# First attention with heads 32 partitions apart, fp32 products on four parts of the array, and packed weights

## The reference

```python
def _feature_map(x, fm_w, fm_b):                 # per head of 8: 16 features
    z = jnp.einsum('nshd,ed->nshe', x, fm_w) + fm_b
    return jnp.concatenate([jnp.exp(z), jnp.exp(-z)], axis=-1)
v, k, q = (_feature_map(t, fm_w, fm_b) for t in (v, k, q))       # 16 heads
scores = jnp.einsum('nqhd,nkhd->nhqk', q, k) / jnp.sqrt(jnp.float32(EMBED))
attn = jax.nn.softmax(scores, axis=-1)
out = jnp.einsum('nhql,nlhd->nqhd', attn, v).reshape(N, S, HEADS * EXP_DIM)
return out @ fc_w.T + fc_b
...
x = x + _L0_xattn_ref(ctx, ctx, _layernorm(x), ...)   # the part above
x = x + _L0_ffn_ref(_layernorm(x), ...)               # 8 experts of 64, weighted, dense
x = x + _L1_xattn_ref(_layernorm(x), ctx, ctx, mask, ...)
x = x + _L1_ffn_ref(_layernorm(x), ...)               # top 2 of 8 experts of 512
```

## Time and profile before

| what | us |
|---|---|
| three runs | 460.05, 459.45, 459.58 (median 459.58) |
| span of the profiled execution (the page has no other time of it) | 460.0 |
| TensorE busy | 372.7 (81%) |
| VectorE busy | 252.0 (55%) |
| GpSimd busy | 175.7 (38%) |
| ScalarE busy | 150.5 (33%) |
| mean granted clock of TensorE | 0.857 of full speed |

### The profile page before, as it was taken

The page is one execution under the profiler, slowest core; times in us unless marked ns, Lnnn a source line. Parts: engine busy times, 40 slices in busy tenths (PEclk is TensorE's granted clock), DMA queues, the critical chain, the costliest instruction groups (busy, mean ns, idle before and its releaser), DMA issues.

```text
span 460.0 us, 6601 instructions
## 1 busy us (share of the span) xinstructions
PE 372.7 (81%) x2130; PEld 290.7 (63%) x2131; DVE 252.0 (55%) x708; ACT 150.5 (33%) x267; POOL 175.7 (38%) x211
## 2 busy tenths in 40 slices
PE   3851879999999999699999598414999999999910
PEld 2421758787887884356558487402788888888800
DVE  5999633426465045551353979588355454545414
ACT  2462522323323225221121556110244343444413
POOL 5999980001010010400111511325466666666322
PEclk9987779999899599655999979655799999999965
DMA  5500000000000001500000444100111111112064
GB/s 146 119 1 0 2 0 1 0 1 0 1 2 0 1 0 41 166 1 0 2 0 1 137 118 135 46 1 13 29 47 51 42 49 43 48 43 48 23 171 120
DMA packets 29352, 18.97 MB, mean 41 GB/s; under 512 B 6683, under 2 KB 27055, under 8 KB 29327
## 3 DMA queue, kind: packets, MB, share of 16 engines
q1 hardware_dynamic: 26831, 13.53, 10.6%
q0 software_dynamic: 2496, 5.12, 4.0%
HBM read 13.99 MB, written 4.65 MB: 41 GB/s over the span
## 4 chain that ended last, share of the span: by engine, by line
PE 68%; DVE 23%; DMA 2%; issue 2%; POOL 2%; ACT 1%; SPq 1%; DVEq 0%; ACTq 0%; POOLq 0%
PE ps L1150 58%; PE ps L1573 4%; DVE xn L556 3%; DVE kbhi L624 3%; DVE qlo L630 3%; DVE stats L544 2%; PE ps L1322 1%; DMA dnT<-y_dram 1%; DVE uplo L797 1%; PE ps L1548 1%; DVE x L806 1%; PE ps L1279 1%; DVE mv L547 1%; PE ps L1450 1%; DVE x L962 1%
## 5 line engine op out<-in xcount | busy, mean ns | idle before, releaser
L390 POOL TENSOR_SCALAR rstd<-mv 128x4 f32<-128x4 f32 x16 | 4.0, 251 | 200.6 <-DVE mv L547 200.6
L504 POOL DMA_INDIRECT y_dram<-yb,dst_row x39 | 38.4, 984 | 33.4 <-DVE yb L937 33.4
L640 DVE TENSOR_REDUCE mx<-ps 128x8 f32<-128x616 f32 x32 | 25.6, 799 | 46.3 <-PE ps L1150 46.0
L1042 ACT ACTIVATE ex<-ps 128x512 f32<-128x512 f32 (+1 forms) x40 | 23.9, 597 | 76.4 <-PE ps L1150 76.4
L498 POOL DMA_INDIRECT xg<-xn_dram,src_row x39 | 37.9, 972 | 16.5 <-PE ps L1548 9.3
L1150 PEld LDWEIGHTS ps<-Vx,ex 128*128 128x128 f32 (+1 forms) x320 | 41.7, 201 | 0.9
L1150 PE MATMUL ps<-dnT,hhT 128*128 x312 | 41.4, 276 | 0.6 <-DVE yb L937 0.6
L1150 PE MATMUL ps<-Vx,ex 128*128 128x51 f32 (+2 forms) x320 | 41.5, 278 | 0.0
L1150 PEld LDWEIGHTS ps<-dnT,hhT 128*128 128x128 f32 x312 | 37.9, 192 | 4.1 <-issue 0.8
L1118 ACT ACTIVATE gl<-ps 128x512 f32<-128x512 f32 x39 | 23.3, 597 | 47.0 <-PE ps L1150 47.0
L1150 PE MATMUL ps<-uphi,xghi 128*128 x78 | 35.2, 451 | 0.9 <-DVE xghi L923 0.6
(11 more groups left out here) (262 smaller groups left out, 786.7 us busy)
## 6 DMA issues: line engine op xcount, KB each, us to landing
upn<-in_L_ffn_gate_up_w_dram SPq DMA_DIRECT2D x8, 512.0 KB, 4.2
dnn<-in_L_ffn_down_w_dram SPq DMA_DIRECT2D x8, 256.0 KB, 4.9
dnT<-y_dram SPq DMA_DIRECT2D x8, 256.0 KB, 4.9
x<-in_x_dram SPq DMA_DIRECT2D x4, 256.0 KB, 3.7
xn_dram<-xn SPq DMA_DIRECT2D x4, 256.0 KB, 2.3
out_dram<-x SPq DMA_DIRECT2D x4, 256.0 KB, 2.3
xg<-xn_dram,src_row POOLq DMA_INDIRECT x39, 2.5
y_dram<-yb,dst_row POOLq DMA_INDIRECT x39, 2.2
```

The lines of the kernel that those rows point to most:

```text
L504: g.indirect_dma_start(y_dram, bass.IndirectOffsetOnAxis(ap=dst_row[:, k:k + 1], axis=0), yb[:, k % 2, :], None).then_inc(scattered[k % 2] ...
L640: v.tensor_reduce(mx[:, b % 2, i, half * HH:half * HH + HH].rearrange("p (a h) -> p a h", a=2), ps[:, pair:pair + 2, 0:HK // 2].rearrange( ...
L1042: s.activation(ex[0:rows, m % RING, :], bank[1 + m % 2][0:rows, :], ACT.Exp, scale=SCALE).then_inc(act_ex, 1)
```

## The change

Constants and SyncE first, then the engines. Heads come in 4 groups of 4 per batch, each head on 32 partitions of its own: 16 features, and behind them rows that are 1 since their weights are zero (exp of 0). In `qs` row 16 of each head is overwritten by the negated maximum, which comes by DMA from `mT`. Scores of a head are then one fp32 product of 17 rows into a bank of its own (77 keys by 512 queries); four heads stand on four row parts of the array. Values are one fp32 product per head with 32 columns of weights, four heads on four column parts, all into bank 6; ScalarE copies them to `oT`, TensorE turns them back, VectorE normalises. Maxima still use one fp32r product on all rows, with rounded queries `qh` and spread keys `kb`, 308 columns per product. Weights are laid out ahead of the launch and loaded as `pack0`, `pack1` and `pack2`; `ctx` comes turned. The folding of the second attention's weights moves from set-up to the last batch of the loop.

```diff
-NJ = 2 * NC
-LAG = 2
-RING = 5
-STEPS = NB * NJ + LAG
+RING = 4
+STEPS = NB * NG
+MAX_SPLIT = ((0, 3, 6), (6, 9, 11), (11, 14, 16), (16, 16, 16))
...
+            for b in range(NB):
+                sp.wait_ge(act_mT, b + 1)
+                for g in range(NG):
+                    sp.dma_start(qs[FD:P:R, b, g, :], mT[GH * g:GH * g + GH, b % 2, :]).then_inc(shifted[b % 2][g], 16)
```

GpSimd, set-up:

```diff
+            layernorm_rstd(0, 0)
+            layernorm_rstd(0, 1)
+            g.wait_ge(act_kst, NG)
+            spread_keys(1)
+            layernorm_rstd(0, 2)
+            round_queries(1)
+            layernorm_rstd(0, 3)
```

VectorE, set-up:

```diff
+            layernorm_apply(0, 0)
+            v.wait_ge(act_kst, NG)
+            v.tensor_tensor(kb[:, 0, :, :].bitcast(F32R).rearrange("p g (j k) -> p g j k", j=GH),
...
+            layernorm_apply(0, 1)
+            for n in range(HEADS // 2):
+                max_of(0, n)
+            v.wait_ge(ld_x[2], 16)
+            layernorm_stats(2)
+            for n in range(HEADS // 2, HEADS):
+                max_of(0, n)
+            layernorm_apply(0, 2)
+            v.wait_ge(ld_x[3], 16)
+            layernorm_stats(3)
+            layernorm_apply(0, 3)
```

ScalarE, set-up and loop:

```diff
+            queries(0, qh[:, 0], act_qh)
+            queries(0, qs[:, 0], act_qs)
+            copy_xT(0, 1, bank[6])
+            queries(1, qs[:, 1], act_qs)
...
+                        s.activation(ex[:, p % RING, :, :], ps[0:KEYS, 2 * h:2 * h + 2, :], ACT.Exp, scale=SCALE).then_inc(act_ex, 1)
+                if G >= 1:
+                    copy_oT(G - 1)
```

TensorE, set-up and loop (`NG` is 4 groups, `GH` 4 heads, `R` 32 partitions, `GK` 308, `FD` 16; `Wz` is a part of `pack0`):

```diff
+            def spread(src, cols, n):
+                for g in range(NG):
+                    ins = mm(bank[g][:, 0:n], Wz[R * g:R * g + R, :], src[R * g:R * g + R, cols])
+                return ins
-                mm(o, sel[:, half, cols], nmT[:, b % 2, :], True, False)
-                mm(o, kbhi[:, b, half, cols], qhi[:, b, half, :], False, False)
-                mm(o, kblo[:, b, half, cols], qhi[:, b, half, :], False, False)
-                mm(o, kbhi[:, b, half, cols], qlo[:, b, half, :], False, True).then_inc(pe_sc, 1)
+            def scores(G):
+                b, g = divmod(G, NG)
+                pe.wait_ge(shifted[b % 2][g], 16 * (b // 2 + 1))
+                if G >= 1:
+                    pe.wait_ge(act_ex, 2 * G)
+                else:
+                    pe.wait_ge(act_qs, NG * NB)
+                for j in range(GH):
+                    rows = slice(R * j, R * j + FD + 1)
+                    ins = mm(bank[j][0:KEYS, :], kst[rows, g, b * KEYS:(b + 1) * KEYS], qs[rows, b, g, :])
+                    if j % 2:
+                        ins.then_inc(pe_sc, 1)
+            def values(G):
+                b, g = divmod(G, NG)
+                pe.wait_ge(act_ex, 2 * G + 2)
...
+                for j in range(GH):
+                    ins = mm(bank[6][R * j:R * j + R, :], Vx[:, b, g * P + R * j:g * P + R * j + R],
+                             ex[:, (2 * G + j // 2) % RING, j % 2, :])
+                ins.then_inc(pe_av, 1)
+            for G in range(STEPS + 2):
+                b, g = divmod(G, NG)
+                if G < STEPS:
+                    scores(G)
+                if b + 1 < NB:
+                    for n in range(MAX_SPLIT[g][0], MAX_SPLIT[g][1]):
+                        max_job(b + 1, n)
+                if 1 <= G <= STEPS:
+                    values(G - 1)
+                if G >= 2:
+                    turn_values(G - 2)
...
```

More of the change, by code:

```diff
@@ L21 @@
 HEADS, HD, FD = 16, 8, 16
-HH = HEADS // 2
-HK = HH * KEYS
-NC = -(-HK // P)
+GH = 4
+NG = HEADS // GH
+GK = GH * KEYS
+R = P // GH
 E0, H0 = 8, 64
@@ L54 @@
 LOOP1 = LOOP0 + (NBLK - 1 - LOOP0) // UNROLL * UNROLL
[L57 to L78, removed]
 def two_layer_kernel(nc, A, out):
@@ L425, in _ @@
[L425 to L431, removed]
-                                    wide(kf[:, half, b * KEYS:(b + 1) * KEYS].unsqueeze(1), P, HH, KEYS),
-                                    wide(maskK[:, :].unsqueeze(2), P, HH, KEYS), ALU.mult).then_inc(pool_kbf, 1)
@@ L440, in _ @@
+            layernorm_rstd(0, 0)
[5 more added lines that the diff above has]
+            layernorm_rstd(0, 3)
+            for b in range(2, NB):
+                spread_keys(b)
+            round_queries(2)
             add_bias(0)
@@ new lines, in queries, with copy_mT, copy_oT @@
+            def queries(b, dst, signal):
+                s.wait_ge(pe_z, b + 1)
+                for g in range(NG):
+                    s.activation(dst[:, g, :], bank[g], ACT.Exp, bias=bz[:, 0:1], scale=sgn).then_inc(signal, 1)
+            def copy_mT(b):
+                s.wait_ge(pe_nmT, b + 1)
+                s.activation(mT[:, b % 2, :], bank[4][0:HEADS, :], ACT.Copy, scale=-1.0).then_inc(act_mT, 1)
+            def copy_oT(G):
+                s.wait_ge(pe_av, G + 1)
+                if G >= 2:
+                    s.wait_ge(pe_T, G - 1)
+                s.activation(oT[:, G % 2, :], bank[6], ACT.Copy).then_inc(act_oT, 1)
@@ L1156, in transpose_xn @@
                 ins.then_inc(pe_xT, 1)
+            def spread(src, cols, n):
+                for g in range(NG):
+                    ins = mm(bank[g][:, 0:n], Wz[R * g:R * g + R, :], src[R * g:R * g + R, cols])
+                return ins
+            pe.wait_ge(ld_l0, 16)
+            pe.wait_ge(ld_ctx, 16)
+            spread(ctxT, slice(0, NB * KEYS), NB * KEYS).then_inc(pe_kz, 1)
             pe.wait_ge(pool_ident, 1)
-            pe.wait_ge(ld_ctx, 16)
+            pe.wait_ge(act_kst, NG)
@@ L1231, in turn_nm, with queries @@
-            def turn_nm(b):
-                pe.wait_ge(dve_nm, b + 1)
-                if b >= 2:
+                for g in range(NG):
+                    ins = pe.transpose(bank[4 + b][0:KEYS, g * P:(g + 1) * P], kst[:, g, b * KEYS:(b + 1) * KEYS], ident[:, :])
+                ins.then_inc(pe_vt, 1)
+            def queries(b):
+                pe.wait_ge(xT_ready, b + 1)
+                if b >= 1:
+                    pe.wait_ge(act_qs, NG * b)
+                spread(xnT[:, b, :], slice(0, SEQ), SEQ).then_inc(pe_z, 1)
@@ L1255, in gate_logits, with turn_on @@
-            def gate_logits(b, last):
+                    ins = pe.transpose(bank[7][:, i * P:(i + 1) * P], oT[:, G % 2, i * P:(i + 1) * P], ident[:, :])
+                ins.then_inc(pe_T, 1)
+            def turn_on(b, pair, dst):
+                for i in range(2):
+                    for a in range(2):
+                        at = (2 * i + a) * P
+                        ins = pe.transpose(dst[:, at:at + P], on[:, b % 2, 2 * pair + i, a * P:(a + 1) * P], ident[:, :])
+                ins.then_inc(pe_onT, 2)
@@ L1256, in gate_logits, with project @@
+            def project(b, dst):
+                pe.wait_ge(ld_w, 16)
+                pe.wait_ge(act_onT, (b + 1) * NI)
+                for i in range(NI):
+                    for a in range(2):
+                        ins = mm(dst[:, i * D:(i + 1) * D], onT[:, i, a, :], fcT[:, a, :], a == 0, a == 1)
+                ins.then_inc(pe_fc, 1)
+            def gate_logits(b, last, dst):
                 pe.wait_ge(ld_small, 16 * N_SMALL)
@@ new lines, in _ @@
+            transpose_xn(0, 0, bank[0])
+            queries(0)
+            pe.wait_ge(act_vx, 3)
+            transpose_xn(0, 1, bank[6])
+            queries(1)
+            for n in range(HEADS // 2):
+                max_job(0, n)
+            for n in range(HEADS // 2, HEADS):
+                max_job(0, n)
+            turn_max(0)
+            pe.wait_ge(act_vx, NB)
+            transpose_xn(0, 2, bank[7])
+            queries(2)
+            pe.wait_ge(xT_ready, 2)
+            transpose_xn(0, 3, bank[6])
@@ new lines, in _ @@
+            queries(3)
+            for G in range(STEPS + 2):
+                b, g = divmod(G, NG)
+                if G < STEPS:
+                    scores(G)
+                if b + 1 < NB:
+                    for n in range(MAX_SPLIT[g][0], MAX_SPLIT[g][1]):
+                        max_job(b + 1, n)
+                if 1 <= G <= STEPS:
+                    values(G - 1)
+                if G >= 2:
+                    turn_values(G - 2)
+                if b + 1 < NB:
+                    for n in range(MAX_SPLIT[g][1], MAX_SPLIT[g][2]):
+                        max_job(b + 1, n)
+                    if g == 2:
+                        turn_max(b + 1)
+                if 1 <= b < NB and g >= 2:
+                    pe.wait_ge(dve_on, G - 1)
+                    turn_on(b - 1, g - 2, bank[7])
+                if b >= 2 and g == 0:
+                    pe.wait_ge(dve_on, G - 1)
+                    project(b - 2, bank[7])
+                if b == NB - 1:
+                    fold(g)
+                    if g == 0:
+                        pe.wait_ge(dve_max, HEADS * NB)
+                        transpose_xn(1, 0, bank[5])
+                    elif g == 2:
+                        pe.wait_ge(act_lg, 1)
+                        transpose_xn(1, 1, bank[5])
+                    else:
```

(3 more changed lines are left out.)

708 lines of the change are left out of this document (268 added, 440 removed).

## The result

The changed kernel takes 470.06 us (median of 4 runs, 469.23 to 471.66) against 459.81 for the kernel before on the same chip: ratio 1.0232, 95% interval 1.0203 to 1.0261. It is slower, by 10 us; the forecast was 424. The profiled execution has a span of 468.9.

What follows compares the result with a forecast made beforehand. VectorE's set-up chain to 60.7 us, then TensorE's first attention, were taken as bounds. First score at 41, loop 86 and 5, then 5.2 and 0.3 put the gates' copy at 139.5, 35.4 earlier: 460.0 to 424.6, forecast 424, range 408 to 482.

Steps and rivals of the forecast that it cites:

- The loop: First attention's 16 groups: 48 for twelve, 12.6 around them, 25.6 for the last batch, 86 us, plus 5 for shapes.
- signs of being wrong: Set over 1.9 us, loop clock at 0.5, or first scores after 50 because GpSimd's rounding holds back `rstd`.
- Set of four at 0.96, full overlap: Loop: four fp32 products on different array parts run together in 0.96 us; one after another would be 3.84.
- B: Rival: parts overlap by half, because records start strictly in order; a set takes 2.4 us, kernel 473; chance 0.28.
- C: Rival: no overlap between array parts, 106 us more, 530 or 520 with some on waits; chance 0.09.
- Change of shape, 0 to 0.17 each: Loop: changing array shapes four times a group, 64 in all, costs 0 to 11 us; 5 taken.
- The group, 4.0: Loop: 0.96 scores, 0.96 values, 0.49 transposes and 1.6 maxima make 4.0 us per group of four heads.
- A: The forecast itself: four parts at once, 424 us, own range 408 to 442; chance 0.54.
- D: Rival: four parts at once but loop at half clock, groups of 6.4 instead of 4.0 us, kernel 467; chance 0.09.
- The loop at full clock: From first score at 41 to last normalisation at 134 us, with 5 for changes of shape.
- First score, 41: End of set-up: first score at 41 us, 20 earlier than before, with GpSimd's rounding of at most 5.5 just hidden.
- From the last normalisation to the gates' copy: After the loop: 17 small gate operations and an apply, 5.2, and 0.3 more; copy at 139.5 us.

Runs made afterwards that it cites:

- e6: Changed kernel with heads 0 and 2 of every score and value set left out: 492.74 us, one run.
- e8: Changed kernel with GpSimd's keys and queries after the applies, 36 bf16 fillers before the first score, and scores on 32 rows: 438.44 us, ratio 0.9527.
- e10: e9 with VectorE's small gate operations moved behind the last normalisation and behind the products with batch 0's gates: 426.28 us, ratio 0.9449.
- e5: Changed kernel with GpSimd's spreading and rounding of batches 2 and 3 waiting until VectorE has applied all four batches' normalisation: 476.53 us.
- e9: e8 with one more filler behind each of the first batch's 16 maximum products and four instead of eight before the last transposes: 433.36 us.
- e1: Changed kernel with score products on 32 rows instead of 17, the added rows holding ones: 442.83 us, ratio 0.9591.
- e7: Changed kernel with GpSimd's keys and queries after the applies and 36 bf16 fillers before the first score, scores on 17 rows: 472.31 us, ratio 1.0279.
- e3: Changed kernel with four bf16 filler products on 128 rows ahead of each value set: 460.78 us, ratio 0.999.
- e4: Changed kernel with four bf16 filler products on 17 rows ahead of each value set: 503.69 us, ratio 1.0937.
- e12: e1's kernel timed again, beside the unedited changed kernel (469.6 us) on the same chip: 442.78 us, ratio 0.9777.

## Why the prediction was wrong

The failed step is one premise under **The loop**: the group's prices were taken at full clock. The overlap was right; the clock alone turned the direction. Three of the prediction's signs of being wrong came: a set over 1.9 us, a loop at 0.5, and first scores after 50, though not by the rounding that it named. Point by point, against its sum:

- **Set of four at 0.96, full overlap.** Right: 1.00 to 1.09 at full clock, and e6's two products cost the same. B and C, 0.37 of the chances, are refuted. By the program-order rule that the prediction cited (the Trainium skill, TensorE: Matmul & The Clock Gate, Packing small matmuls) the second record of one part would hold up the next, and a set would take 2.4; the trace disagrees with that, 1.00 for eight records.
- **Change of shape, 0 to 0.17 each.** 1.09 and 1.00 against 0.96 bound it at 0.13, and e8's groups (1.03 and 1.00) at 0.07. If all 64 cost the mean of e8's two excesses, 0.055, they are 3.5 us, an estimate; 5 was taken. The drain of which the Trainium skill speaks (TensorEngine Tiling (Array Packing), Key Properties) costs no more than this at the two changes that lead into a set; the others weren't measured.
- **The group, 4.0.** A group of e8 takes 3.8 at full clock (51.04 to 54.87), one of the changed kernel 6.4 at half (57.30 to 63.66), near the figures of A and D.
- **The clock: +37.1.** From first score to last normalisation: 133.9 in the changed kernel, 96.8 in e8 with the same list at nearly full clock (1.00 to 120 us, 0.93 behind it). D had this, and a chance of 0.09. That its 467 lies so near is in part luck: it has 12 us for half clock in the last four groups, of which three had full clock, and nothing for the late first score. Its evidence was at hand: the earlier trace rows had fp32 products at half clock with TensorE never idle. That busy share does not by itself hold the clock up was written down, and the loop was priced at full clock all the same.
- **The loop at full clock: +3.8.** 96.8 in e8 against the forecast's 93, and this hides two errors. The first twelve groups with what stands around them were forecast at 60.6 and took 60.7 (47.33 to 108.08), and the 5 for changes of shape wasn't needed on top. From there to the last normalisation it is 36.1 against 27.4, 8.7 more: small gate operations, one slowed by GpSimd, stand ahead of the last normalisations; e10 shows 5.9 to be had there. The working looked only behind the last normalisation.
- **First score, 41: +11.0.** GpSimd beside the last apply (e5: 3.3 of it at the first score), then the half clock from 20 us on (e9: another 4.1, with the clock at 0.94). The remaining 3.6 wasn't traced to single steps. GpSimd's rounding, which had been the feared one, was short: 1.89 against at most 5.5.
- **From the last normalisation to the gates' copy: -0.8** (4.7 against 5.5). **Behind it: -6.8.** 278.3 against 285.1 us; the dense layer's half clock lasted 14 us instead of 28, though the apply of 4.94 came again.

11.0 + 37.1 + 3.8 - 0.8 - 6.8 = 44.3, which is 468.9 - 424.6.

## What to carry to other kernels

Packing small fp32 products on parts of the array multiplies the work per time almost fully (four in 1.00 to 1.09 us, one in 0.96), but price it at both clocks before believing the gain: here such a group cost 3.8 or 6.4 us. Use all 32 rows of a part when the added ones leave the result as it is; here they held ones, whose constant the softmax cancels, it cost no time in a set and gave 27 us. Zeros weren't tried. When a step frees an engine, list what its neighbour then starts: GpSimd's wide operations, moved beside VectorE's applies, made one apply 6.4 us longer.

## What the runs showed of the hardware

- In this loop rows in use, not TensorE's waits, decided the clock: 17 rows 0.50, 32 rows 1.00, with equal durations at equal clock (e1, e7, e8); bf16 fillers on 128 rows raised it, on 17 they didn't (e3, e4). Rows that hold nothing but ones count.
- Rows aren't the whole rule. With 17 rows the clock was full for some us behind a projection on 128 rows (121.90) and in the last batch. With products nearly all on 64 to 128 rows, and TensorE never idle, the kernel before had 0.50 from 190 to 218. e1 and e12, the same kernel, rose near 95 and near 78 us. No run explains when the clock changes.
- VectorE beside GpSimd: an apply of 1.11 us took 7.49 (e5 shows that GpSimd was the cause), a small operation of 0.19 took 2.36 (seen beside it, not tested alone).
- The loop over the experts has two lengths, 121 and 131 us (e6 and e8 have 131, e9 has 121), across executions of unchanged instructions; its cause wasn't looked for.
